# Attention hands over normalised token-major rows; the FFN's bias is added by VectorE

## What is computed

```python
x = L0_attn_x                                    # (4, 2048, 512) float32
q, k, v = (x @ W.T, split into 16 heads of 32)   # Wq, Wk, Wv
attn = softmax(q @ k.T / sqrt(32)) @ v           # per head, all 2048 keys
x = layernorm(x + attn)                          # no gain or bias
w = where(weights >= 0, 1, -1)
y = clip((x @ w.T) * scale + bias, -100, 100)
out = layernorm(x + y)
```

## Time and profile before

| | |
|---|---|
| median of three runs | 2723.47 us (2723.27 to 2724.31) |
| profiled execution, its own time | 2722.63 us |
| its span, first to last instruction | 2720.5 us |
| project | about 0 to 552 us |
| attend | about 552 to 2438 us |
| normalise_and_ffn | about 2438 to 2720 us |
| busy, of the whole span | PE 99%, PEld 58%, DVE 81%, ACT 83%, POOL 23% |
| mean granted TensorE clock | 0.994 of full speed |

### The profile page before, as it was taken

How to read it: one execution, slowest core, us unless ns; L and a number is a source line. 1 busy time by engine, 2 the same in 40 slices (tenths; PEclk the granted TensorE clock), 3 DMA queues, 4 the chain that set the end, 5 groups by cost and what they waited for, 6 DMA issues and landing times.

```text
span 2720.5 us, 92280 instructions
## 1 busy us (share of the span) xinstructions
PE 2685.3 (99%) x38720; PEld 1581.4 (58%) x38720; DVE 2193.1 (81%) x2623; ACT 2260.5 (83%) x2726; POOL 615.2 (23%) x661
## 2 busy tenths in 40 slices
PE   9999999999999999999999999999999999979998
PEld 8888888744454444444444444445455544447887
DVE  7444444379989989989989989989998998978998
ACT  5333333399999999999999999999999999965665
POOL 1000000012222222222222222222222222225665
PEclk9999999999999999999999999999999999989999
DMA  6555555589898999989899898999989899975553
GB/s 230 191 195 193 186 186 186 197 170 199 172 208 176 200 188 193 202 168 210 172 199 194 179 207 175 199 184 199 194 173 206 177 201 187 184 178 176 190 189 136
DMA packets 262711, 513.33 MB, mean 189 GB/s; under 512 B 20674, under 2 KB 135362, under 8 KB 260164
## 3 DMA queue, kind: packets, MB, share of 16 engines
q0 software_dynamic: 73440, 267.42, 52.4%
q1 hardware_dynamic: 179108, 222.61, 25.4%
q10 hardware_dynamic: 9792, 17.83, 1.7%
HBM read 122.43 MB, written 117.96 MB: 88 GB/s over the span
## 4 chain that ended last, share of the span: by engine, by line
PE 97%; DVE 1%; ACT 1%; issue 1%; DMA 0%; SPq 0%; POOL 0%; ACTq 0%; POOLq 0%; DVEq 0%
PE banks L637 34%; PE banks L669 33%; PE banks L228 19%; PE banks L1021 7%; PE banks L690 2%; PE banks L1010 1%; PE banks L1003 1%; PE banks L1017 1%; PE banks L250 0%; PE banks L1004 0%; PE banks L256 0%; DMA scratch_v<-v_out 0%; DMA score_rows<-scratch_k_lo 0%; ACT y L1039 0%; DVE qk_raw L357 0%
## 5 line engine op out<-in xcount | busy, mean ns | idle before, releaser
L780 ACT ACTIVATE probs<-banks 128x1024 f32<-128x1024 f32 x2048 | 1877.5, 1781 | 4.1 <-PE banks L637 4.1
L637 PE MATMUL banks<-score_rows 97*32 97x512 f16 x16384 | 1259.4, 382 | 4.9 <-POOL den_in L595 3.9
L669 PE MATMUL banks<-probs,v_keys 128*32 128x256 f32 x16384 | 1251.6, 379 | 0.5 <-ACT probs L780 0.5
L609 POOL DMA_DIRECT2D total<-partial x510 | 439.0, 861 | 1439.2 <-DVE partial L835 498.6
L835 DVE TENSOR_TENSOR partial<-partial,probs 128x1024 f32<-128x1024 f32 x640 | 748.4, 1221 | 0.0
L669 PEld LDWEIGHTS banks<-probs,v_keys 128*32 128x32 f32 x16384 | 510.5, 110 | 405.8 <-ACT probs L780 0.9
L831 DVE TENSOR_TENSOR partial<-probs 128x1024 f32<-128x1024 f32 x512 | 604.2, 1222 | 119.9 <-issue 109.7
L637 PEld LDWEIGHTS banks<-score_rows 97*32 97x32 f16 x16384 | 351.4, 95 | 509.7 <-ACT probs L780 413.2
L356 DVE TENSOR_TENSOR qk_lo<-banks,qk_hi 128x512 f16<-128x512 f32 x128 | 88.4, 691 | 241.7 <-ACT qk_hi L311 241.6
L311 ACT ACTIVATE qk_hi<-banks 128x512 f16<-128x512 f32 x128 | 76.0, 594 | 185.2 <-PE banks L228 185.2
L228 PE MATMUL banks<-xT_hi,w_hi 128*128 128x512 f32 x512 | 197.6, 390 | 0.0
(11 more groups left out here) (95 smaller groups left out, 2180.4 us busy)
## 6 DMA issues: line engine op xcount, KB each, us to landing
total<-partial POOLq DMA_DIRECT2D x510, 512.0 KB, 6.2
scratch_q_raw<-qk_raw SPq DMA_DIRECT2D x16, 1024.0 KB, 5.7
scratch_k_raw<-qk_raw SPq DMA_DIRECT2D x16, 1024.0 KB, 5.7
scratch_v<-v_out SPq DMA_DIRECT2D x16, 1024.0 KB, 5.1
score_rows<-scratch_q_hi SPq DMA_DIRECT2D x128, 128.0 KB, 5.5
score_rows<-scratch_k_hi SPq DMA_DIRECT2D x128, 128.0 KB, 4.3
v_keys<-scratch_v SPq DMA_DIRECT2D x64, 256.0 KB, 7.0
scratch_attn<-wf_scaled SPq DMA_DIRECT2D x64, 256.0 KB
```

Of the source, the lines that this page charges most:

```text
L609: pool.dma_start(total[:, qb % 2, heads], partial[:, g - 1, heads], accum_op=ALU.add).then_inc(a_merge[qb % 2][pair], 16)
L637: last = nc.tensor.matmul(scores_of(phase, unit)[part, i, :], k_rows[:, h, keys], q_rows[:, h, qb * BLK:(qb + 1) * BLK], start=True, stop= ...
L669: last = nc.tensor.matmul(banks[rows, out_bank(qb), cols], v_keys[:, kt, rows], probs[:, kt % P_RING, h, cols], start=(kt == 0 and part == ...
L780: nc.scalar.activation(probs[:, kt % P_RING, heads, :], scores_of(it % SLOTS, qb * UNITS + u), ACT.Exp, scale=SCALE / GAIN ** 2).then_inc( ...
```

## The change

In `attend` the output copy is turned to token-major by four transposes behind key tile 4 of the next block (`turn_output`), copied again (`copy_turned`), and the denominators are summed with a `select` matrix, which has a column of ones for the piece, so that the four pieces share 128 columns of the bank; their tiles are 8, 9, 10 and 11. VectorE copies the denominators after tile 12, TensorE turns them with one transpose after tile 13, VectorE takes the reciprocal (after tile 14) and multiplies (`normalise`, after tile 15); SP stores the normalised rows, in pieces of 512 bytes, to a token-major `dram["attn"]`. `dram["den"]` is gone. `a_dout`, for which `values` waits, now comes from the reciprocal.

In the FFN stage the transposes of attention and denominators, the reciprocal and the product are gone; GpSimd adds the loaded rows to x. The bias product is gone: VectorE adds `bias_b` (the bias, loaded once to all partitions) out of PSUM into `biased`, does both bn_stats, and then clips from SBUF to SBUF. TensorE's next product in the bank waits for `biased`. A block is loaded by four transfers, one for each tile.

```diff
 P_RING = 8
 SLOTS = 3
 LAG = 2
-DEN_TILES = (8, 10, 12, 13)
-DEN_EDGES = (0, 128, 256, 384, BLK)
-OUT_AFTER = 2
-DEN_AFTER = 13
+DEN_TILES = (8, 9, 10, 11)
+TURN_TILE = 4
+DEN_TURN_TILE = 13
+OUT_AFTER, TURNED_AFTER, DEN_AFTER, INVERT_AFTER, NORMAL_AFTER = 2, 5, 12, 14, 15
 
 
...
+            sp.wait_ge(a_norm, it * QB + qb + 1)
+            dst = dram["attn"].rearrange("n g (b c q) f -> (n g) b q c f", b=QB, q=P)[bass.ds(it, 1), qb]
+            src = normal[:, qb % 2, :].rearrange("q (c f) -> q c f", c=TPB)
+            sp.dma_start(dst.rearrange("o q c f -> (o q) c f"), src).then_inc(a_store[qb % 2], 16)
 
...
 
+        def turn_output(it, qb):
+
+            st = it * QB + qb
+            pe.wait_ge(a_out, st + 1)
+            for c in range(TPB):
+                cols = slice(c * P, (c + 1) * P)
+                last = nc.tensor.transpose(banks[:, out_bank(qb), cols], out_sb[:, cols], ident2[:])
+            last.then_inc(a_turn, 1)
...
         def denominators(it, qb, piece):
+
             st = it * QB + qb
-            cols = slice(DEN_EDGES[piece], DEN_EDGES[piece + 1])
+            cols = slice(piece * P, (piece + 1) * P)
...
             for part in parts:
                 for h in range(G):
                     rows = slice(HD * h, HD * h + HD)
-                    last = nc.tensor.matmul(banks[rows, out_bank(qb), cols], ones[:], part[:, h, cols],
-                                            start=(part is parts[0]), stop=(part is parts[-1]))
+                    last = nc.tensor.matmul(banks[rows, out_bank(qb), 0:P], select[:, piece, :], part[:, h, cols],
+                                            start=(piece == 0 and part is parts[0]),
+                                            stop=(piece == TPB - 1 and part is parts[-1]), skip_group_check=True)
             last.then_inc(a_den, 1)
+
+        def turn_denominators(it, qb):
+
+            pe.wait_ge(a_dcopy, it * QB + qb + 1)
+            nc.tensor.transpose(banks[:, out_bank(qb), P:2 * P], den_sb[:], ident2[:]).then_inc(a_dturn, 1)
+
+        def behind(it, qb, kt):
+
+            if kt == TURN_TILE:
+                turn_output(it, qb)
+            if kt in DEN_TILES:
+                denominators(it, qb, DEN_TILES.index(kt))
+            if kt == DEN_TURN_TILE:
+                turn_denominators(it, qb)
 
...
-                if kt in DEN_TILES and qb > 0:
-                    denominators(it, qb - 1, DEN_TILES.index(kt))
-                elif kt in DEN_TILES and not (isinstance(it, int) and it == 0):
-                    denominators(it - 1, QB - 1, DEN_TILES.index(kt))
+                if qb > 0:
+                    behind(it, qb - 1, kt)
+                elif kt < HEAD and not (isinstance(it, int) and it == 0):
+                    behind(it - 1, QB - 1, kt)
 
...
-            nc.vector.tensor_copy(out_sb[:, parity, :], banks[:, out_bank(parity), :]).then_inc(a_out, 1)
+            dve.wait_ge(a_turn, st)
+            nc.vector.tensor_copy(out_sb, banks[:, out_bank(parity), :]).then_inc(a_out, 1)
+
+        def copy_turned(st, parity):
+            dve.wait_ge(a_turn, st + 1)
+            dve.wait_ge(a_norm, st)
+            nc.vector.tensor_copy(turned, banks[:, out_bank(parity), :]).then_inc(a_turned, 1)
 
         def copy_den(st, parity):
             dve.wait_ge(a_den, (st + 1 + 2) * len(DEN_TILES))
-            dve.wait_ge(a_store[parity], (st - parity) * 16 + 32)
-            nc.vector.tensor_copy(den_sb[:, parity, :], banks[:, out_bank(parity), :]).then_inc(a_dout, 1)
+            dve.wait_ge(a_dturn, st)
+            nc.vector.tensor_copy(den_sb[:], banks[:, out_bank(parity), 0:P]).then_inc(a_dcopy, 1)
+
+        def invert_den(st, parity):
+            dve.wait_ge(a_dturn, st + 1)
+            dve.wait_ge(a_norm, st)
+            src = banks[:, out_bank(parity), P:2 * P].rearrange("q (h c) -> q h c", h=G)[:, :, 0:TPB]
+            nc.vector.reciprocal(rden[:].rearrange("q c h -> q h c"), src).then_inc(a_dout, 1)
+
+        def normalise(st, parity):
+            dve.wait_ge(a_dout, st + 1 + 2)
+            dve.wait_ge(a_store[parity], (st - parity) * 8 + 16)
+            nc.vector.tensor_tensor(normal[:, parity, :].rearrange("q (k d) -> q k d", d=HD),
+                                    turned.rearrange("q (k d) -> q k d", d=HD),
+                                    rden[:].rearrange("q c h -> q (c h)").unsqueeze(2).to_broadcast([P, TPB * G, HD]),
+                                    ALU.mult).then_inc(a_norm, 1)
 
         def item(it, first):
...
+                    if kt == DEN_AFTER:
+                        copy_den(st - 1, (qb - 1) % 2)
+                    if kt == INVERT_AFTER:
+                        invert_den(st - 1, (qb - 1) % 2)
+                    if kt == NORMAL_AFTER:
+                        normalise(st - 1, (qb - 1) % 2)
+
                 for kt in range(KT):
                     if kt in EDGES:
+                        finish_last(kt)
                         continue
                     g = next(i for i in range(GROUPS) if kt < EDGES[i + 1])
...
@@ -980,9 +1037,9 @@
             if t is not None:
                 if s % TPB == 0:
                     pool.wait_ge(f_x[s // TPB], r * 16 + 16)
-                pool.wait_ge(f_attn, t + 1 + 2)
+                    pool.wait_ge(f_in[s // TPB], r * 16 * TPB + 16 * TPB)
                 pool.wait_ge(f_y[0], t + 1)
-                nc.gpsimd.tensor_tensor(res1[:, s % 2], attn[:, s % 2], x_in[:, s // TPB, s % TPB], ALU.add).then_inc(f_res[0], 1)
+                nc.gpsimd.tensor_tensor(res1[:, s % 2], attn[s // TPB][:, s % TPB], x_in[:, s // TPB, s % TPB], ALU.add).then_inc(f_res[0], 1)
 
         all_steps(pool, step)
...
-            t, s = tile(r, j, ATTN)
-            if t is not None:
-                k = s // TPB
-                cols = slice(s % TPB * P, (s % TPB + 1) * P)
-                if s % TPB == 0:
-                    pe.wait_ge(f_in[k], r * 32 + 32)
-                pe.wait_ge(f_attn, t + 1)
-                for c in range(DC):
-                    nc.tensor.transpose(aT_bank(s)[:, c * P:(c + 1) * P], attnT[k][:, c, cols], ident3[:])
-                nc.tensor.transpose(banks[:, 6 + s % 2, 0:P], den_in[k][:, cols], ident3[:]).then_inc(f_aT, 1)
...
             t, s = tile(r, j, FFN)
             if t is not None:
                 pe.wait_ge(f_ylo, t + 1 + 2)
-                pe.wait_ge(f_clip, t + 1)
-
-                nc.tensor.matmul(ffn_bank(s), bias_ones[:], bias_rows[:], start=True, stop=False)
+                pe.wait_ge(f_biased, t + 1)
                 for c in range(DC):
                     cols = slice(c * P, (c + 1) * P)
                     for part, w in ((yT_hi, wf_hi), (yT_lo, wf_hi), (yT_hi, wf_lo)):
-                        last = nc.tensor.matmul(ffn_bank(s), part[:, s % 4, cols], w[:, c, :], start=False,
...
@@ -1104,24 +1150,17 @@
             t, s = tile(r, j, CLIP)
             if t is not None:
                 dve.wait_ge(f_ffn, t + 1 + 4)
-                dve.wait_ge(f_res[1], t + 1 - 2 + Y_SLOTS)
-                nc.vector.tensor_scalar(clipped[:, s % 2], ffn_bank(s), -MAX_VAL, MAX_VAL, ALU.max, ALU.min).then_inc(f_clip, 1)
+                dve.wait_ge(f_clip, t + 1)
+                nc.vector.tensor_tensor(biased[:, s % 2], ffn_bank(s), bias_b[:], ALU.add).then_inc(f_biased, 1)
             for t, s, which in norms:
                 statistics(t, s, which, (res1, res2)[which], (2 * TPB, Y_SLOTS)[which])
-            attn_t, attn_s = tile(r, j, ATTN)
-            if attn_t is not None:
-                dve.wait_ge(f_aT, attn_t + 1)
-                dve.wait_ge(f_attn, attn_t + 1)
-                nc.vector.reciprocal(rden[:, attn_s % 2], den_bank(attn_s)).then_inc(f_rden, 1)
+            t, s = tile(r, j, CLIP)
+            if t is not None:
+                dve.wait_ge(f_biased, t + 1 + 2)
+                dve.wait_ge(f_res[1], t + 1 - 2 + Y_SLOTS)
+                nc.vector.tensor_scalar(clipped[:, s % 2], biased[:, s % 2], -MAX_VAL, MAX_VAL, ALU.max, ALU.min).then_inc(f_clip, 1)
             for t, s, which in norms:
                 aggregate(t, s, which)
-            if attn_t is not None:
-
-                dve.wait_ge(f_rden, attn_t + 1)
-                dve.wait_ge(f_res[0], attn_t + 1 - 2 + 2 * TPB)
-                nc.vector.tensor_tensor(attn[:, attn_s % 2].rearrange("p (h d) -> p h d", h=H),
-                                        aT_bank(attn_s).rearrange("p (h d) -> p h d", h=H),
-                                        rden[:, attn_s % 2].unsqueeze(2).to_broadcast([P, H, HD]), ALU.mult).then_inc(f_attn, 1)
...
```

## The result

The changed kernel takes 2766.45 us (median; 2765.54 to 2767.71) against 2723.37 us for the kernel before on the same chips: a ratio of 1.016 (95% interval 1.0145 to 1.0176), 43 us slower. The forecast was 2761 us.

What follows compares the result with a forecast made beforehand. ScalarE was taken to bound attention, with TensorE's spare 0.72 us a block, and TensorE the FFN. Attention +20, the FFN's ring +17 and ends 0 make +37, giving 2761 us, range 2737 to 2792.

Steps and rivals of the forecast that it cites:

- Attention becomes TensorE's: Attention: TensorE needs 29.66 us per block against ScalarE's 29.34, so it becomes the bound, +20 us over 63 blocks.
- The price of a tiling change: Attention, TensorE: leaving the 128*32 tiling and coming back costs 0.25 us, twice per block, 0.50 us.
- Rival A: Attention: the tiling switches hide, 0.1 us or less a trip; attention +1, FFN +17, 2741 us; chance 0.17.
- The ring through GpSimd: FFN: clip, GpSimd's res2 and res1, and two stats wait in a circle; 4.31 us a step against 4.01, +17 us.
- Rival B: FFN: the ring doesn't bind and the step stays at about 3.97 to 4.01 us; 2743 us; chance 0.10.
- rival D: Clip and stats cost as out of PSUM, a tiling trip over 0.3 us: up to +39 +33, 2795 us; chance 0.10.
- VectorE's own path: FFN: VectorE's sequence from clip through the stats takes 3.97 us a step, below the ring's 4.31.
- The ends: Attention's tail and the FFN's start: about +3 and -3 us, together 0, bounds -3 and +5.
- the FFN's first steps give about 3 us back: FFN start: without reciprocal and product before res1, 0.6 us saved for each of five steps, about 3 us.
- Rival F: FFN: the smaller loads come late, +12 to +180 us; chance 0.03.
- Rival E: FFN: TensorE's clock stays at 1.2 GHz because it idles, +127 us more, some 2890 us; chance 0.03.
- Rival C: FFN: falls to VectorE's bare work, 3.36 us a step, -38 us; 2706 us or below; chance 0.07.

Runs made afterwards that it cites:

- experiment 5: Changed kernel with the denominators turned by four 128*32 products side by side in place of one 128*128 transpose: 2756.09 us, ratio 1.0121 to the kernel before.
- experiment 6: Changed kernel with one output transpose behind each of key tiles 4 to 7, what follows moved later: 2812.06 us, ratio 1.0326 to the kernel before.
- Experiment 1: Changed kernel with GpSimd adding res1 before res2 in the FFN: 2746.62 us, ratio 1.0089 to the kernel before.
- experiment 3: Kernel before with only the FFN's bias edit (bias addition, stats, then clip; no bias product), attention as before: 2739.20 us, ratio 1.0059.

## Why the prediction held, step by step

**Attention becomes TensorE's** (forecast +20, measured +26): right, and by the named cause. The price of a tiling change, carried over from L250 in the projection as 0.25, was 0.26 and 0.30 in place. The block came out at 29.75 instead of 29.66; the two trips make 0.06 of the 0.09, and 63 blocks make 6 us of it. This is the largest part of what the forecast missed. ScalarE's idle time was put at 0.3 us a block; it is 0.1, and another 0.3 lies inside its busy time. Rival A (the switches hide) is ruled out by experiments 5 and 6. The Trainium skill (TensorEngine Tiling (Array Packing), Key Properties) says that changing the tiling mode drains the engine. The trace agrees in that each trip costs 0.25 to 0.30 us and no weight load runs ahead over it.

**The ring through GpSimd** (forecast 4.31 us a step and +17, measured 4.27 for 4.02, +14): right. Experiment 1 opens it by an order alone. The term that was too large is GpSimd's pair: its second addition starts 1.25 us behind the first, where the duration of 1.29 was counted. Clip took 0.41 us, 0.42 was estimated. The Trainium skill (VectorE: DVE Perf Modes, Mode 2×_2P) says that a float32 operation with one input tensor makes two results a cycle within SBUF and can't do so out of PSUM. The trace agrees: from start to start clip takes 0.33 us (2601.23 to 2601.56), and out of PSUM it took 0.61 (2554.16 to 2554.77). Rival B falls with experiments 1 and 3, rival D with this clip and the trips of 0.26 and 0.30.

**VectorE's own path** was given as 3.97 us; with the ring open (experiment 1) the step is 3.94.

**The ends** (forecast 0, bounds -3 and +5, measured +4.4): the step "the FFN's first steps give about 3 us back" failed. The tail came out at +4.4 for +3, and x_res 0.8 later where no change was forecast. From the first res1 to the first pair of stats the FFN takes 20.2 us (2477.44 to 2497.67) where it took 20.8 (2445.51 to 2466.33): 0.6 back, not 3. From the third res1 on, the additions wait for the normalised tile of ScalarE instead of the attn product:

```profile
2477.44 2.48 POOL L1042 TENSOR_TENSOR res<-attn,x_res 128x512 f32<-128x512 f32 x2 [7.35 <-DMA x_res<-in_x]
...
2482.87 1.27 POOL L1042 TENSOR_TENSOR res<-attn,x_res 128x512 f32<-128x512 f32 x1 [2.95 <-ACT y L1084]
```

**Costed at nothing, and rightly:** the 512-byte pieces (the FFN's loads land after 3.7 us, and no addition waits for them in the steady part), SP's later stores, VectorE's five operations per block (it waits 1.4 us for the last piece, at most 1.9, where under 1 was forecast, but TensorE doesn't wait for it). Rival F (loads too late) didn't occur. Rival E didn't occur: the granted clock is 1.00, the upper level of 2.4 GHz, in the FFN's window although TensorE idles 43 of 230 us. Rival C's 3.36 us a step was not reached by any order tried here; 3.49 was, with TensorE the bound.

## What to carry to other kernels

Work that is taken from a full engine pays only if the next bound is lower, and the next bound may be no engine but a ring: before moving an operation to a later place in its engine's order, follow who waits for it and what stands behind that waiter in its own queue. Where a stage's two busiest engines both look full, find which one has spare time per round, and compare all that is added, changes of tiling included, with that spare. Put small products of another shape into the tiling that surrounds them, even at twice their array time.

## What the runs showed of the hardware

Leaving the 128*32 tiling for 128*128 and coming back cost 0.26 us around four transposes and 0.30 around the single one (changed kernel), and 0.25 around a single one in experiment 6. The other way round, 128*128 to 128*32 and back around L250, it cost 0.25. Between neighbours of the same tiling weights were loaded 0.21 us ahead of their products; over a change they were not. Doubling a turn's array time within the tiling made the kernel 10 us faster (experiment 5). From 2510 to 2740 us the granted clock was 1.00 with TensorE busy for 186.7 of 230 us, idle for 0.8 in each step of 4.27.
